# Expert matrices loaded with consecutive rows on a partition, in an eight-stage soft-MoE behind two graph convolutions

## The chip, the core and the metric

One core of one Trainium2 chip runs the whole program. The metric is the device time of one execution in microseconds (us). Engines are TensorE (PE; its weight loads are shown apart as PEld), VectorE (DVE), ScalarE (ACT), GpSimd (POOL) and SyncE (SP), which here only issues transfers. Transfers run on the core's 16 DMA engines.

## The reference

Two graph convolutions (6250 nodes, 768 channels, 100000 edges and the self loops), then a soft mixture of experts. The part around the change, cut from the reference:

```python
d_w = jax.nn.softmax(logits, axis=-1)                       # over the 32 slots of an expert
c_w = jax.nn.softmax(logits.reshape(b, l, E * S), axis=-1)  # over all 1024 slots
slots = jnp.einsum('bld,bles->besd', xn, d_w)
h = jax.nn.gelu(jnp.einsum('besd,edh->besh', slots, w1) + b1[:, None, :], approximate=False)
eo = jnp.einsum('besh,ehd->besd', h, w2) + b2[:, None, :]
return jnp.einsum('bkd,blk->bld', eo.reshape(b, E * S, d), c_w)
```

There are E = 32 experts of S = 32 slots. w1 is 32 x 768 x 384 and w2 is 32 x 384 x 768, both float32: 1.18 MB for each matrix of each expert, 75.5 MB together.

## The kernel before

The program runs in phases with a barrier between them: `prepare`, `constants`, `first_layer` (first convolution), `second_layer` (second convolution, logits, both softmaxes, sums of the slots), `experts` and `combine`. Rows of 128 nodes make a block; there are 49 blocks (NBR).

**second_layer.** Per block PE does 17 steps of four matmuls for the convolution (line 1370: 512 and 256 columns in turn, weights `pick[:, i % 2, :, t]`, read with a stride of 18 float16 elements, 36 bytes), 36 matmuls for the logits (line 1398), 12 transposes (lines 1414 and 1422) and, for the sums of the slots, six units (line 1385, `unit(n)`). A unit makes one 128 x 512 piece of `slots` for two blocks: six matmuls of 512 columns whose weights are 128 columns of the normalised rows `xn`. There are 12 units for each of 24 pairs of blocks, and 12 shorter ones for the last block, 300 in all. DVE adds each result to `slots` (line 1257). `slots[p, c, k]` holds channel d = c * 128 + p of slot k, since the unit for chunk c takes the columns c * 128 to c * 128 + 127 of `xn`. Units stand between the steps of the convolution, so nearly always behind a matmul of 256 columns.

**Loads of the first four experts.** SP issues w1 of experts 0 to 3 in round NBR + 1 of its loop (line 1168) and w2 of experts 0 to 3 behind the loop (line 1183).

**experts.** Four experts (G) make a group; there are eight groups. Per group PE does `up` (line 1545: 24 matmuls of float32 by w1, on 32 columns of the array each), three transposes of the activated `hb` (line 1553) and `down` (line 1562: 24 matmuls by w2). Up of group i is placed ahead of the transposes and down of group i - 1. ACT's order is: scaled slots `sl`, Gelu of group i (line 1504), copy `hT` of group i - 1 (line 1508). DVE adds the first bias for group i (line 1522) and the second for group i - 1 (line 1526).

The loads come from SP alone, in this order for group i: four first biases (line 1480), four second biases (line 1483), four w1 of group i + 1 (line 1472, once up of group i - 1 has freed the buffer), then, once down of group i - 1 is done (w2 has one buffer), four w2 of group i (line 1490). A bias is one row of HBM that is written to 32 partitions. All of these go through one queue in order, so the biases of group i + 1 lie behind w2 of group i.

w1 of one expert is loaded as `"(c p) h -> p c h"`: six pieces of 384 float32 (1536 bytes) for each partition. w2 is loaded as `"(c p) d -> p c d"`: three pieces of 768 float32 (3072 bytes).

**combine** multiplies the experts' outputs by the combine weights, 49 blocks of 48 matmuls.

Of the kernel before, what the change touches and what calls it, by code (L numbers as in the profile page):

```python
# [12 lines left out]
P = 128  # L13
# [3 lines left out]
DC = D // P  # L17
# [19 lines left out]
HC = H // P  # L37
# [1018 lines left out]
                    steps(14, CT)  # L1056


def second_layer(nc, table, idx, dloc, tab, dinv_g, brow, valid, phi_h, phi_l, scl, slots, ident16, iota_x, x_pad, x2_dram, cw_dram,
                 rows_mem, sums_mem, w1, w2, w1_first, w2_place, w1_in, w2_in):  # L1060

    with ExitStack() as ctx:
# [6 lines left out]
        def sb(name, shape, dt):  # L1069
            return ctx.enter_context(nc.sbuf_tensor("m_" + name, shape, dt))  # L1070

        RING = 14
        XN = 6
        DW = 4
# [12 lines left out]
        xn = sb("xn", [P, XN, 2, D], F16)  # L1087
# [3 lines left out]
        dw = sb("dw", [P, DW, 2, K], F16)  # L1091
# [15 lines left out]
        ps_s = ctx.enter_context(nc.psum_tensor("m_ps_s", [P, 2, 512], F32))  # L1107
# [40 lines left out]
        with nc.Block() as block:  # L1148
            @block.sync
            def _(sp):  # L1150
                for i in range(NBR + 3):
                    if i < NBR:
                        b = own_block(sp, tab, i)
                        wait(sp, based, 2 * (i - 1))
                        sp.dma_start(own[:, i % 2, :], table[bass.ds(b * P, P), :]).then_inc(self_in[i % 2], 16)
                    j = i - 2
                    if 0 <= j < NBR:
                        b2 = own_block(sp, tab, j)
                        sp.wait_ge(x2_r, j + 1)
                        sp.dma_start(x2_dram[bass.ds(b2 * P, P), :], xb[:, j % 2, :]).then_inc(x2_out[j % 2], 16)  # L1160
                    if i < NBR:
                        wait(sp, xn_f, i - 1)
                        wait(sp, x2_out[i % 2], 16 * (i // 2))
                        sp.dma_start(xb[:, i % 2, :], x_pad[bass.ds(b * P, P), :]).then_inc(x_in[i % 2], 16)
                    if i == NBR + 1:
                        sp.wait_ge(consumed, NT)
                        for q in range(G):
                            sp.dma_start(w1_first[:, q], w1[q].rearrange("(c p) h -> p c h", p=P)).then_inc(w1_in[q], 16)
                    k = i - 3
                    if 0 <= k < NBR:  # L1170
                        b3 = own_block(sp, tab, k)
                        sp.wait_ge(cw_hi, k + 1)
                        sp.wait_ge(cw_lo, k + 1)
                        sp.dma_start(cw_dram[bass.ds(b3 * P, P), :], cst[:, :]).then_inc(cw_out, 16)
                sp.wait_ge(x2_out[0], 16 * ((NBR + 1) // 2))
                sp.wait_ge(x2_out[1], 16 * (NBR // 2))
                sp.wait_ge(evicted, 2 * NBR)
                sp.wait_ge(zeroed, NBR)
                sp.wait_ge(scaled_u, 3 * NBR)
                sp.wait_ge(xn_f, NBR)  # L1180
                sp.wait_ge(xn_lo, NBR)
                for q in range(G):
                    sp.dma_start(w2_place[:, q], w2[q].rearrange("(c p) d -> p c d", p=P)).then_inc(w2_in[q], 16)
                sp.wait_ge(cw_out, 16 * NBR)

            @block.gpsimd
# [168 lines left out]
            @block.tensor  # L1355
            def _(pe):
                for i in range(last):
                    j, k = i - 1, i - 2

                    def steps(first, stop):  # L1360
                        if i >= NBR:
                            return
                        for t in range(first, stop):
                            n = CT * i + t
                            pe.wait_ge(gathered[n % RING], 16 * (n // RING + 1))
                            bit = pe.snap((w >> t) & 1)
                            to = (pe.snap(bit << 9), pe.snap(bit << 8))
                            for half in range(2):
                                for (at, f, e), off in zip(OWN, to):
                                    mm = nc.tensor.matmul(part[:, bass.ds(off + at, e - f)], pick[:, i % 2, :, t],  # L1370
                                                          ring[:, n % RING, half * D + f:half * D + e],
                                                          start=False, stop=(t == CT - 1 and half == 1), skip_group_check=True)
                            mm.then_inc(consumed, 1)

                    def unit(n):
                        g, u = group_unit(i, n)
                        if g is None:
                            return
                        bins = bins_of(g)
                        c, a = u // 2, 512 * (u % 2)  # L1380
                        pe.wait_ge(dw_lo, bins[-1] + 1)
                        wait(pe, added, UNITS * g + u - 1)
                        for q in bins:
                            for xh, dh in ((0, 0), (0, 1), (1, 0)):
                                mm = nc.tensor.matmul(ps_s[:, u % 2, :], xn[:, q % XN, xh, c * P:(c + 1) * P], dw[:, q % DW, dh, a:a + 512],  # L1385
                                                      start=(q == bins[0] and xh == 0 and dh == 0), stop=(q == bins[-1] and xh == 1))
                        mm.then_inc(unit_r, 1)

                    if i < NBR:
                        w = pe.value_load(tab[0:1, 4 * i:4 * i + 1], min_val=0, max_val=2 ** CT)  # L1390
                    if 0 <= k < NBR:
                        pe.wait_ge(xt_hi, k + 1)
                        pe.wait_ge(xt_lo, k + 1)
                        wait(pe, lg_r, k)
                        for c in range(DC):
                            for half, ph in ((0, phi_h), (0, phi_l), (1, phi_h)):
                                for a in (0, 512):
                                    mm = nc.tensor.matmul(ps_l[:, a:a + 512], xT[:, half, c * P:(c + 1) * P], ph[:, c, a:a + 512],  # L1398
                                                          start=(c == 0 and half == 0 and ph is phi_h), stop=(c == DC - 1 and half == 1))
                        mm.then_inc(logits, 1)  # L1400
                    if i < NBR:
                        pe.wait_ge(wiped, i + 1)
                        pe.wait_ge(picked, i + 1)
                    steps(0, 2)
                    unit(0)
                    steps(2, 5)
                    unit(1)
                    steps(5, 8)
                    unit(2)
                    if 0 <= j < NBR:  # L1410
                        pe.wait_ge(xn_hi, j + 1)
                        wait(pe, xt_lo, j)
                        for c in range(DC):
                            mm = nc.tensor.transpose(ps_t[:, c * P:(c + 1) * P], xn[:, j % XN, 0, c * P:(c + 1) * P], ident16[:, :])
                        mm.then_inc(hi_turned, 1)
                    steps(8, 11)
                    unit(3)
                    if 0 <= j < NBR:
                        pe.wait_ge(xn_lo, j + 1)
                        pe.wait_ge(xt_hi, j + 1)  # L1420
                        for c in range(DC):
                            mm = nc.tensor.transpose(ps_t[:, c * P:(c + 1) * P], xn[:, j % XN, 1, c * P:(c + 1) * P], ident16[:, :])
                        mm.then_inc(lo_turned, 1)
                    steps(11, 14)
                    unit(4)
                    steps(14, CT)
                    unit(5)


def experts(nc, w1, eb1, w2, eb2, slots, eo, mxs, ident16, w1_first, w2s, w1_in, w2_in):  # L1430


    with ExitStack() as ctx:
# [13 lines left out]
        ident32 = sb("ident32", [P, P], F32)  # L1447
        sl = sb("sl", [P, 2, DC, P], F32)
        hb = sb("hb", [P, 2, H], F32)
        hT = sb("hT", [P, H], F32)  # L1450
        ps_h = ctx.enter_context(nc.psum_tensor("e_ph", [P, 2, 512], F32))
        ps_g = ctx.enter_context(nc.psum_tensor("e_pg", [P, 512], F32))
# [6 lines left out]
        n = NG // 2 + 1  # L1459
        eb1_v = eb1.rearrange("(g j) (o h) -> g j o h", j=G, o=1)  # L1460
        eb2_v = eb2.rearrange("(g j) (o h) -> g j o h", j=G, o=1)
        w1_v = w1.rearrange("e (c p) h -> p e c h", p=P)
        w2_v = w2.rearrange("e (c p) d -> p e c d", p=P)


        with nc.Block() as block:
# [67 lines left out]
            def _(pe):  # L1534
                def body(j):
                    for s in range(2):
# [11 lines left out]
                        if exists(i - 1, NG):  # L1548
# [1 line left out]
                            pe.wait_ge(act_r, i)  # L1550
                            wait(pe, back, i - 1)
                            for c in range(HC):
                                mm = nc.tensor.transpose(ps_g[:, c * P:(c + 1) * P], hb[:, 1 - s, c * P:(c + 1) * P], ident32[:, :])
                            mm.then_inc(turned, 1)
                            pe.wait_ge(back, i)
                            wait(pe, eo_r, i - 2)
# [135 lines left out]
```

## Time and profile before

| | us |
|---|---|
| median of 3 runs | 3592.69 |
| lowest and highest | 3588.29, 3596.18 |
| the profiled execution, its own time | 3595.14 |
| its span | 3593.4 |
| second_layer, logits and sums of slots, about | 1555 to 2966 |
| experts, from the first bias load to the last down | 2967.8 to 3190.3 |
| combine | from 3193 |

The span is what the profiler records between first and last instruction; 1.7 us of the execution lie around it. PE is busy for 88% of the span, the DMA queues with 53.3% and 27.3% of the 16 engines' time. Starts of instructions are counted from the start of the span.

### The profile page before, as it was taken

The page shows a single profiled execution, that of the slowest core. Times are in us where ns is not written, and L with a number is a line of the kernel's source. Part 1 is how long each engine was busy: PE and PEld are TensorE (multiplying, and loading weights), DVE is VectorE, ACT ScalarE, POOL GpSimd, SP SyncE. Part 2 cuts the span into 40 slices and gives each one's busy share as a digit, 9 for nine tenths or more (in the row PEclk, how much of TensorE's full clock was granted, in tenths as well). Part 3 has the DMA queues.
Part 4 walks back from the last instruction along what each step waited for, and adds up shares of the span by engine and source line. Part 5 has one row for each costly group of instructions (what it writes and reads, how often), then busy time and mean ns, then how long its engine had stood idle before and what let it go on. Part 6 is the DMA issues. An engine that isn't in the chain of part 4 may idle for free. (4 is left out here: it accounts for less than half of the span.)

```text
span 3593.4 us, 60125 instructions
## 1 busy us (share of the span) xinstructions
PE 3161.1 (88%) x19503; PEld 1984.9 (55%) x19503; DVE 1954.4 (54%) x2997; ACT 1176.2 (33%) x1414; POOL 1820.1 (51%) x1692
## 2 busy tenths in 40 slices
PE   7214999999999999969999999999999984469998
PEld 6212666666666666635555555555555541136665
DVE  7865444444444444338888888887888870111111
ACT  6662222222222222214444444444444430000000
POOL 0104777777777777467666666666666600000000
PEclk9997999999999999979999999999999997779999
DMA  9364999999999999579888888888888849956665
GB/s 376 123 270 153 323 327 311 307 310 309 304 313 308 306 312 309 198 252 350 300 299 306 305 303 300 299 306 302 305 296 305 304 173 324 354 179 173 164 172 140
DMA packets 360335, 994.09 MB, mean 277 GB/s; under 512 B 139458, under 2 KB 168412, under 8 KB 360080
## 3 DMA queue, kind: packets, MB, share of 16 engines
q0 software_dynamic: 133728, 656.12, 53.3%
q1 hardware_dynamic: 226352, 334.57, 27.3%
q8 instruction: 160, 2.62, 0.3%
q14 instruction: 95, 0.78, 0.1%
HBM read 841.95 MB, written 122.89 MB: 269 GB/s over the span
## 5 line engine op out<-in xcount | busy, mean ns | idle before, releaser
L1191 POOL DMA_INDIRECT rows_mem<-table,idx x833 | 915.1, 1099 | 480.3 <-PE m_part L1370 239.8
L900 POOL DMA_INDIRECT rows_mem<-table,idx x833 | 883.7, 1061 | 346.6 <-issue 179.2
L1370 PE MATMUL m_part<-rows_mem,sums_mem 128*128 128x512 f16 (+1 forms) x3332 | 600.6, 330 | 28.9 <-DMA rows_mem<-table,idx 24.7
L1023 PE MATMUL a_part<-rows_mem,sums_mem 128*128 128x512 f16 (+1 forms) x3332 | 581.2, 328 | 49.0 <-DMA rows_mem<-table,idx 44.4
L1370 PEld LDWEIGHTS m_part<-rows_mem,sums_mem 128*128 128x128 f16 x3332 | 422.6, 142 | 176.5 <-issue 42.7
L1023 PEld LDWEIGHTS a_part<-rows_mem,sums_mem 128*128 128x128 f16 x3332 | 414.1, 142 | 177.3 <-issue 58.3
L1385 PE MATMUL m_ps_s<-m_dw,m_xn 128*128 128x512 f16 x1764 | 429.5, 380 | 28.2 <-DVE slots L1257 26.7
L1398 PE MATMUL m_ps_l<-phi_mem,m_xT 128*128 128x512 f16 x1764 | 388.7, 379 | 0.1
L1665 PE MATMUL c_po<-c_eh,c_cT 128*128 128x512 f16 (+1 forms) x1568 | 320.7, 327 | 7.4 <-DMA c_cT<-cw_dram 7.4
L1398 PEld LDWEIGHTS m_ps_l<-phi_mem,m_xT 128*128 128x128 f16 x1764 | 172.5, 98 | 208.0 <-issue 0.4
L1385 PEld LDWEIGHTS m_ps_s<-m_dw,m_xn 128*128 128x128 f16 x1764 | 167.0, 98 | 214.4 <-issue 56.0
L1004 PE MATMUL a_ps_o<-W1h,a_vT 128*128 128x512 f16 (+1 forms) x1176 | 248.3, 327 | 2.0 <-DVE a_vT L986 2.0
L1004 PE MATMUL a_ps_o<-W2h,a_vT 128*128 128x512 f16 (+1 forms) x1176 | 248.8, 327 | 0.9 <-ACT a_vT L936 0.9
L989 DVE SCALAR_TENSOR_TENSOR a_u<-a_ps_o,inv,brow 128x768 f32<-128x768 f32 x49 | 49.9, 1018 | 331.5 <-PE a_ps_o L1004 331.5
L1648 DVE SCALAR_TENSOR_TENSOR c_ob<-c_po,c_inv,c_xb 128x768 f32<-128x768 f32 x49 | 49.8, 1017 | 330.1 <-PE c_po L1665 330.1
L1257 DVE TENSOR_TENSOR slots<-slots,m_ps_s 128x512 f32<-128x512 f32 x288 | 196.4, 683 | 42.2 <-PE m_ps_s L1385 41.5
L1665 PEld LDWEIGHTS c_po<-c_eh,c_cT 128*128 128x128 f16 x1568 | 153.8, 98 | 110.0 <-DMA c_cT<-cw_dram 7.8
L1197 ACT ACTIVATE m_part<-m_zeros 128x1536 f32<-128x1536 f32 x50 | 72.7, 1453 | 373.5 <-DVE sums_mem L1288 365.2
L1665 PE MATMUL c_po<-c_el,c_cT 128*128 128x512 f16 (+1 forms) x784 | 192.2, 327 | 0.0
L933 ACT ACTIVATE sums_mem<-a_u,dinv_s 128x768 f16<-128x768 f32 x49 | 45.9, 937 | 432.1 <-DVE a_u L989 432.1
L1004 PEld LDWEIGHTS a_ps_o<-W1h,a_vT 128*128 128x128 f16 x1176 | 115.3, 98 | 76.6 <-ACT a_vT L930 2.1
L1004 PEld LDWEIGHTS a_ps_o<-W2h,a_vT 128*128 128x128 f16 x1176 | 115.5, 98 | 75.9 <-issue 1.4
(346 smaller groups left out, 3951.4 us busy)
## 6 DMA issues: line engine op xcount, KB each, us to landing
sums_mem<-table SPq DMA_DIRECT2D x98, 384.0 KB, 6.1
sums_mem<-in_L_ffn_w_dram SPq DMA_DIRECT2D x32, 1152.0 KB, 10.3
rows_mem<-table,idx POOLq DMA_INDIRECT x1666, 5.2
cw_dram<-m_cst SPq DMA_DIRECT2D x49, 512.0 KB, 5.6
x_pad<-xs SPq DMA_DIRECT2D x7, 2688.0 KB, 23.9
table<-arena SPq DMA_DIRECT2D x49, 384.0 KB, 2.7
table<-a_stage SPq DMA_DIRECT2D x49, 384.0 KB, 4.2
sums_mem<-x_pad SPq DMA_DIRECT2D x49, 384.0 KB, 5.0
```

The costliest lines, as they stand in the source:

```text
L900: pool.indirect_dma_start(out=ring[:, t, :], out_offset=None, in_=table, in_offset=bass.IndirectOffsetOnAxis(ap=idx[:, k:k + 1], axis=0)). ...
L989: v.scalar_tensor_tensor(u[:, :], ps_o[:, 0:D], inv[:, 0:1], brow[:, :], ALU.mult, ALU.add).then_inc(biased, 1)
L1004: mm = nc.tensor.matmul(ps_o[:, a:z], vT[:, half, c * P:(c + 1) * P], Wp[:, c, a:z], start=(c == 0 and half == 0 and Wp is Ws[0]), stop=(c ...
L1023: mm = nc.tensor.matmul(part[:, bass.ds(to + a, z - a)], pick[:, i % 2, :, t], ring[:, t, half * D + a:half * D + z], start=False, stop=(t ...
L1191: pool.indirect_dma_start(out=ring[:, t, :], out_offset=None, in_=table, in_offset=bass.IndirectOffsetOnAxis(ap=idx[:, n:n + 1], axis=0)). ...
L1197: nc.scalar.activation(part[:, :], zeros[:, :].to_broadcast([P, 3 * 512]), ACT.Copy).then_inc(wiped, 1)
L1257: v.tensor_tensor(slots[:, c, a:a + 512], slots[:, c, a:a + 512], ps_s[:, unit % 2, :], ALU.add).then_inc(added, 1)
L1370: mm = nc.tensor.matmul(part[:, bass.ds(off + at, e - f)], pick[:, i % 2, :, t], ring[:, n % RING, half * D + f:half * D + e], start=False ...
L1385: mm = nc.tensor.matmul(ps_s[:, u % 2, :], xn[:, q % XN, xh, c * P:(c + 1) * P], dw[:, q % DW, dh, a:a + 512], start=(q == bins[0] and xh ...
L1398: mm = nc.tensor.matmul(ps_l[:, a:a + 512], xT[:, half, c * P:(c + 1) * P], ph[:, c, a:a + 512], start=(c == 0 and half == 0 and ph is phi ...
L1648: v.scalar_tensor_tensor(ob[:, s, :], ps_o[:, s, 0:D], inv[:, 0:1], xb[:, s, :], ALU.mult, ALU.add).then_inc(summed, 1)
L1665: mm = nc.tensor.matmul(ps_o[:, s, a:e], cT[:, s, half * KC + c, :], ee[:, c, a:e], start=(c == 0 and half == 0 and ee is eh), stop=(c == ...
```

## The change

The expert matrices are loaded so that consecutive rows stand on one partition: w1 as `"(p c) h -> p c h"` (partition p holds rows 6p to 6p + 5), w2 as `"(p c) d -> p c d"` (rows 3p to 3p + 2). Either is then one piece of 9216 contiguous bytes in HBM and in SBUF for each partition, in place of six or three. What multiplies w1 and w2 has to stand in the same order: chunk c of `slots` becomes the channels d = 6p + c, and chunk c of the transposed activations the hidden units h = 3p + c. Both come from reading the weights of a matmul with a stride (`spread`): 6 float16 elements (12 bytes) in line 1385, and 3 float32 elements (12 bytes) in the transposes of line 1553. The numbers of matmuls, transfers, bytes and waits stay as they are.

```diff
+def spread(rows, n):
+
+    return rows.rearrange("p (d c) -> p c d", c=n)
 ...
-                            sp.dma_start(w1_first[:, q], w1[q].rearrange("(c p) h -> p c h", p=P)).then_inc(w1_in[q], 16)
+                            sp.dma_start(w1_first[:, q], w1[q].rearrange("(p c) h -> p c h", p=P)).then_inc(w1_in[q], 16)
 ...
-                    sp.dma_start(w2_place[:, q], w2[q].rearrange("(c p) d -> p c d", p=P)).then_inc(w2_in[q], 16)
+                    sp.dma_start(w2_place[:, q], w2[q].rearrange("(p c) d -> p c d", p=P)).then_inc(w2_in[q], 16)
 ...
-                                mm = nc.tensor.matmul(ps_s[:, u % 2, :], xn[:, q % XN, xh, c * P:(c + 1) * P], dw[:, q % DW, dh, a:a + 512],
+                                mm = nc.tensor.matmul(ps_s[:, u % 2, :], spread(xn[:, q % XN, xh, :], DC)[:, c, :], dw[:, q % DW, dh, a:a + 512],
 ...
-        w1_v = w1.rearrange("e (c p) h -> p e c h", p=P)
-        w2_v = w2.rearrange("e (c p) d -> p e c d", p=P)
+        w1_v = w1.rearrange("e (p c) h -> p e c h", p=P)
+        w2_v = w2.rearrange("e (p c) d -> p e c d", p=P)
 ...
-                                mm = nc.tensor.transpose(ps_g[:, c * P:(c + 1) * P], hb[:, 1 - s, c * P:(c + 1) * P], ident32[:, :])
+                                mm = nc.tensor.transpose(ps_g[:, c * P:(c + 1) * P], spread(hb[:, 1 - s, :], HC)[:, c, :], ident32[:, :])
```

## Rows read from the trace of the kernel before

**Rows 1.** The page, 40 equal slices of 89.8 us: PE busy in tenths, GB/s.

```profile
PE   7214999999999999969999999999999984469998
GB/s 376 123 270 153 323 327 311 307 310 309 304 313 308 306 312 309 198 252 350 300 299 306 305 303 300 299 306 302 305 296 305 304 173 324 354 179 173 164 172 140
```

**Rows 2.** Timeline, PE, second_layer: start, length (us), line, operation, count.

```profile
2745.42 2.11 PE L1370 MATMUL m_part<-rows_mem,sums_mem 128*128 128x512 f16 x12
2747.37 1.46 PE L1385 MATMUL m_ps_s<-m_dw,m_xn 128*128 128x512 f16 x6
2748.66 2.11 PE L1370 MATMUL m_part<-rows_mem,sums_mem 128*128 128x512 f16 x12
```

**Rows 3.** Timeline of experts, groups 2 and 3; in brackets the idle time before and its releaser.

```profile
3054.77 3.59 SPq L1490 DMA_DIRECT2D sums_mem<-in_L_ffn_w_dram  x4
3061.59 6.09 PE L1545 MATMUL e_ph<-rows_mem,e_sl 128*32 128x384 f32 x48 [6.89 <-DMA rows_mem<-in_L_ffn_w_dram]
3076.60 0.56 DVE L1522 TENSOR_TENSOR e_hb<-e_ph,e_bias 128x384 f32<-128x384 f32 x1 [19.88 <-DMA e_bias<-in_L_ffn_b_dram]
3078.54 6.15 PE L1562 MATMUL e_pe<-sums_mem,e_hT 128*32 128x512 f32 x48 [10.38 <-ACT e_hT L1508]
3084.75 2.67 SPq L1490 DMA_DIRECT2D sums_mem<-in_L_ffn_w_dram  x4
```

**Rows 4.** Windows of 1 us, experts: busy times, PE's granted clock, DMA share, GB/s.

```profile
3053.00:3054.00 1.00, 1.00 (x16) 0.36 (x12) 0.00 (x0) 0.00 (x0) 0.00 (x0) 1.00 1.06 373
3064.00:3065.00 1.00, 1.00 (x12) 0.45 (x8) 0.00 (x0) 0.00 (x0) 0.00 (x0) 0.50 1.03 399
3072.00:3073.00 1.00, 0.00 (x0) 0.00 (x0) 0.00 (x0) 0.00 (x0) 0.00 (x0) 0.77 1.10 207
3087.00:3088.00 1.00, 0.00 (x0) 0.00 (x0) 0.01 (x1) 0.00 (x0) 0.00 (x0) 1.00 1.02 379
3143.00:3144.00 1.00, 0.00 (x0) 0.00 (x0) 0.87 (x2) 0.00 (x0) 0.00 (x0) 1.00 1.07 217
```

**Rows 5.** Windows of 4 us in prepare and constants: x in, x_pad out, phi in.

```profile
32.00:36.00 4.00, 3.60 (x38) 3.33 (x36) 3.59 (x5) 3.07 (x9) 0.00 (x0) 1.00 1.03 402
84.00:88.00 4.00, 3.65 (x37) 3.36 (x36) 3.62 (x6) 4.00 (x9) 0.00 (x0) 1.00 1.03 417
256.00:260.00 4.00, 0.73 (x1) 0.50 (x2) 4.00 (x1) 3.21 (x1) 0.00 (x0) 1.00 1.03 411
```

**Rows 6.** Timeline of experts: first w2 load, first w1 load within, later w2 issues, last down.

```profile
2947.86 2.48 SPq L1183 DMA_DIRECT2D sums_mem<-in_L_ffn_w_dram  x4
2972.49 4.72 SPq L1472 DMA_DIRECT2D e_w1s<-in_L_ffn_w_dram  x4
3001.24 2.50 SPq L1490 DMA_DIRECT2D sums_mem<-in_L_ffn_w_dram  x4
3141.99 2.17 SPq L1490 DMA_DIRECT2D sums_mem<-in_L_ffn_w_dram  x4
3169.44 2.26 SPq L1490 DMA_DIRECT2D sums_mem<-in_L_ffn_w_dram  x4
3183.87 6.39 PE L1562 MATMUL e_pe<-sums_mem,e_hT 128*32 128x512 f32 x48 [14.01 <-DMA sums_mem<-in_L_ffn_w_dram]
```

**Rows 7.** Weight loads by line; ns are min/median/max.

```profile
L1370 PEld LDWEIGHTS m_part<-rows_mem,sums_mem x3332: 139/141/165, 1555.2 to 2900.1; 128*128 128x128 f16 x196
L1385 PEld LDWEIGHTS m_ps_s<-m_dw,m_xn x1764: 95/98/151, 1657.9 to 2965.1; 128*128 128x128 f16 x196
L407 PEld LDWEIGHTS psT<-ident,work x7: 180/230/230, 12.2 to 13.3; 128*128 128x128 f32 x7
L1553 PEld LDWEIGHTS e_pg<-e_ident,e_hb x24: 138/140/143, 2995.4 to 3169.5; 128*128 128x128 f32 x24
```

**Rows 8.** Timeline, a unit that had to wait: its weight loads and its matmuls.

```profile
2758.57 0.99 PEld L1385 LDWEIGHTS m_ps_s<-m_dw,m_xn 128*128 128x128 f16 x6 [0.77 <-issue]
2758.60 1.46 PE L1385 MATMUL m_ps_s<-m_dw,m_xn 128*128 128x512 f16 x6 [0.46 <-DVE slots L1257]
```

## Prediction

> **What bounds the kernel now.** I read the slices of the page first [rows 1]. The reader should see two regimes: from slice 17 to 32 (second_layer) PE is at nine tenths in nearly every slice at about 300 GB/s, and in slices 34 and 35 (experts) PE falls to four tenths while the rate is the highest behind the start, 324 and 354 GB/s. The change touches both: weight reads in the first, transfers in the second.
>
> In second_layer the timeline of PE [rows 2] shows each group of matmuls starting before the recorded end of the one ahead, with nothing between them. This phase is bound by PE, so anything that a matmul of line 1385 waits for longer would be paid in full.
>
> In experts a period runs from one issue of w2 to the next. In [rows 3] it goes: w2 issued at 3054.77; w1 of the next group arrives at 3061.59; the first bias, queued behind w2, arrives at 3076.60; down starts at 3078.54, once Gelu and the copy `hT` are done; down ends and w2 is issued again at 3084.75. All that time the DMA engines have work (share 1.02 to 1.10 in the windows [rows 4]). Three rates are to be seen there: 373 GB/s while w1 moves (pieces of 1536 bytes), 399 while w2 moves (3072 bytes), and for about 6 us a dip to 207 at its lowest while the biases move. Issues lie at 3001.24 and, six periods on, at 3169.44 [rows 6], so 28.03 us each. A group's w1 and w2 are 4.72 MB each: 4.72 / 0.373 = 12.65 us and 4.72 / 0.399 = 11.8 us, together 24.5; the other 3.5 us are the biases' dip.
>
> **How fast 9 KB pieces move.** No transfer of the trace has such pieces. The nearest rows [rows 5]: x in, 3072 bytes, 402 GB/s; x_pad out, 3072 bytes, 417; phi in, 4096 bytes, 411. A fit helps: one of 16 engines moves 1536 bytes at 373/16 GB/s in 65.9 ns and 3072 bytes at 399/16 in 123.2 ns, that is 8.6 ns for a piece and 0.0373 ns for a byte. It gives 406 GB/s at 4096 bytes (411 measured) and 419 at 9216. The best loads and stores measured are 411 and 417. I take 418, with 411 and 430 as ends (the second is the fit with the cost of a piece at nothing, 16 / 0.0373), and 373 as the low end for the case that a long piece has a cost of its own. At 418 a matrix group takes 11.3 us: w1 saves 1.35 us, w2 saves 0.5.
>
> The Trainium skill (DMA: Bandwidth & Descriptors, Specifications) puts the minimum transfer for line rate at 512 B, by which both old sizes are full speed already and this saves nothing. The rows disagree: 373, 399 and 411 GB/s at three sizes above that. The rule's outcome is the third rival.
>
> **What of it reaches the end.** If only the DMA engines set the period, it falls from 28.03 by 1.85 to 26.2. But there is a second limit, the loop through w2's single buffer: issue, about 1.3 us to the first bytes (my reading of the last period, below), w2, biases, DVE, ACT, down, issue. Now the queue still holds w1 when w2 is issued, so that the loop has slack: w2 issued at 3084.75 finds w1 moving until about 3087, where the rate passes 373 [rows 4]. That is 2.2 us after the issue, so 0.9 us of slack. In the last full period there is none: issue at 3141.99 [rows 6], and the window 3143 to 3144 already dips to 217 GB/s [rows 4]. That period, 3141.99 to 3169.44, is 27.45 us long, and so a sample of the loop; with w2 shorter by 0.5 it is 26.95. The loop varies with down, 6.15 us in [rows 3]: PE's granted clock moves between 0.50 and 1.00 in this stage [rows 4].
>
> So a period lands between 26.2 (DMA alone) and 26.95 (loop alone), against 28.03: 1.1 to 1.8 us each. Six periods give 6.5 to 11; I take 8, since a shorter w1 brings the loop to the front in about every second period. Ahead of them lies w1 of group 1, issued at 2972.49 [rows 6]: 1.35 us from the rate. Issuing it took SP 4.72 us for four transfers of 768 pieces; with 128 pieces each the queue fills sooner, 0 to 1.5 us, taken as 0.7. Behind them is the last w2, issued at 3169.44 and there at 3183.87 [rows 6], nothing beside it: 0.45 us. Sum: 8 + 1.35 + 0.7 + 0.45 = 10.5 us, with ends of 7 and 16. The first loads (lines 1168, 1183) run beside second_layer. The later one is issued at 2947.86 [rows 6], has 11.8 us to move and so is there by about 2962, while experts starts at 2967.8: 0. With less for SP to issue, the biases are issued earlier, but they stay behind w2 in the same queue, so 0 again; nobody else waits on SP, and no wait is added or moved.
>
> **What the strided weights cost.** Loads with a stride of 36 bytes take 141 ns (line 1370), contiguous ones 98 (line 1385) [rows 7]. At 12 bytes I expect at most 141. The question is whether 43 ns more show. Line 1370 itself tells: from 2745.42 to 2747.37 [rows 2] twelve matmuls with strided weights, six of 512 and six of 256 columns, take 1.95 us, 2.36 columns/ns; the unit behind them, six contiguous loads and 3072 columns from 2747.37 to 2748.66, runs at 2.38. So strided loads hide even behind matmuls of 256 columns (107 ns), and a unit's loads lie behind its own matmuls of 512 (215 ns), the first behind one of 256. When a unit had to wait, its matmul began 0.03 us after its load began [rows 8], not after its end. I take 0. The upper bound is 43 ns exposed once in each of 300 units, 12.9 us; nothing lets a slower load gain, so there is no bound below 0.
>
> The Trainium skill (SBUF — State Buffer, Door 1: The DMA port swizzle, its note on cachelines) asks for two or more accesses to each 16-byte line for full bandwidth. Twelve bytes give 1.3 to a line, so by it the loads of line 1385 slow down; the trace agrees for 36 bytes (141 against 98 ns [rows 7]) and shows nothing at 12. What a slower load would do to the time is the fourth rival.
>
> The transposes of line 1553 read float32 with 12 bytes: 24 loads of 140 ns [rows 7]. They follow up, which ends at 3067.7, and ACT copies their result only behind the Gelu that the bias released at 3076.60 [rows 3]; with 8 us of cover the cost is 0. Uncovered, 24 loads at the slowest float32 row (230 ns [rows 7]) would cost 24 x 0.09 = 2.2 us.
>
> **The rivals.**
> 1. *The loop is the bound throughout* (faster, or within 0.2%). Periods of 26.95 and no gain from the quicker issue: 6.5 + 1.35 + 0.45, less where down falls to a lower clock more often: 5 to 8, some 6.5 us, 3586. For it: the last period. Against: slack in the others.
> 2. *The engines are the bound throughout.* 11 + 1.35 + 1.5 + 0.45 = 14.3 us, up to 17 at 430 GB/s: 3578. For it: a DMA share above 1 in all six periods.
> 3. *Longer pieces don't move faster* than now: 3592.7. Against it are three rising rates.
> 4. *The strided weights show once a unit*: +12.9 against -10.5, 3595. Against it: [rows 2] and [rows 8].
> 5. *Slower: a strided load outlasts its matmul.* It decides where a load at this stride, together with what it shares, takes more than the 215 ns of a 512-column matmul. The slowest strided float16 load is 165 ns, a float32 one 230 [rows 7]; at 230 each of 1764 matmuls waits 15 ns, 26 us, less 10.5: 3608. The same sign, smaller, would come from 9 KB pieces at 373 GB/s: w2 then loses 0.85 us in seven groups, 6 us, 3599.
>
> **How the numbers follow.** About 0.2% (7 us) is what a measurement of this kernel can tell from no change. Chances: the forecast 0.45; the loop 0.17; the engines 0.13; no faster pieces 0.08; strides once a unit 0.07; slower 0.10 for its two forms. Faster than by 0.2%: nearly all of the forecast (0.42), all of the engines, a third of the loop, 0.61 in all. Slower by more than 0.2%: 0.09. Within: 0.30. The likeliest change is -10.5 us. Against the profiled execution that is 3595.1 - 10.5 = 3584.6; the three runs' median lies 2.4 us lower, so 3582.2, rounded to 3582. The range runs from the engines' end, 3575, to the fourth rival's 3595.
>
> **What the profile after would show.** In one-microsecond windows of experts, w1 and w2 at the same rate near 418 GB/s; if w1 stays at 373, the whole gain is wrong. Issues of line 1490 every 26.2 to 27 us; short stretches in which the DMA engines run dry right after an issue would say that the loop has taken over. Four w1 issued in about 2 us into an empty queue, and no longer 14 us. Weight loads of line 1385 near 141 ns, with a unit still 1.29 us behind twelve matmuls in 1.95; longer ones would mean the fourth or fifth rival. The prediction fails if a unit stretches by more than 30 ns (300 of them, 9 us), or if the biases' dip grows.

## The result, and the profile after

| us | before | after |
|---|---|---|
| median of six runs each | 3594.43 | 3581.99 |
| lowest and highest | 3587.91, 3597.83 | 3579.13, 3583.24 |
| the profiled execution, its span | 3593.4 | 3580.3 |
| from the first w1 issue in experts to the issue of combine's first load (of the combine weights, on SP) | 220.53 | 206.83 |

The ratio is 0.9967 (95% interval 0.9954 to 0.998), 12.4 us off the medians, 7 to 17 us by the interval. Of all executions reported in this document one is left out, of the experiment a2, which took 5758.5 us at a granted clock of 0.58. All lines of the code behind the new helper have moved down by five: 1385 is now 1390, 1472 is 1477, 1480 is 1485, 1490 is 1495, 1545 is 1550, 1553 is 1558 and 1562 is 1567.

The page of after, the same slices as [rows 1], and one of its groups (line, engine, tile, count; busy us and mean ns; idle before them):

```profile
PE   7214999999999999969999999999999984469998
GB/s 376 125 271 152 327 325 304 310 310 306 309 311 305 310 310 309 215 243 347 298 308 294 305 300 304 303 297 305 302 307 299 298 174 338 382 180 169 166 171 140
...
L1390 PE MATMUL m_ps_s<-m_dw,m_xn 128*128 128x512 f16 x1764 | 433.1, 383 | 27.0 <-DVE slots L1262 26.9
```

Slices 34 and 35 now move 338 and 382 GB/s, against 324 and 354. Nothing else stands out of the noise. The matmuls of the units last 383 ns on average, 380 before.

One period of experts in the timeline of after, to be laid beside [rows 3]:

```profile
3051.22 2.06 SPq L1495 DMA_DIRECT2D sums_mem<-in_L_ffn_w_dram  x4
3055.86 5.77 PE L1550 MATMUL e_ph<-rows_mem,e_sl 128*32 128x384 f32 x48 [4.71 <-DMA rows_mem<-in_L_ffn_w_dram]
3069.57 0.56 DVE L1527 TENSOR_TENSOR e_hb<-e_ph,e_bias 128x384 f32<-128x384 f32 x1 [16.40 <-DMA e_bias<-in_L_ffn_b_dram]
3071.51 6.61 PE L1567 MATMUL e_pe<-sums_mem,e_hT 128*32 128x512 f32 x48 [9.34 <-ACT e_hT L1513]
3078.18 1.96 SPq L1495 DMA_DIRECT2D sums_mem<-in_L_ffn_w_dram  x4
```

It has the same shape. w2 is issued, up starts, the bias arrives late, down runs and w2 is issued again. The period is 26.96 us here, and was 29.98 in [rows 3]. Windows of the same period (busy times of PE, PEld, DVE, ACT, POOL; PE's granted clock; DMA share; GB/s), as [rows 4]:

```profile
3054.00:3063.00 9.00, 6.31 (x51) 2.84 (x51) 0.00 (x0) 0.00 (x0) 0.00 (x0) 0.81 1.01 427
3063.00:3067.00 4.00, 0.00 (x0) 0.00 (x0) 0.00 (x0) 0.00 (x0) 0.00 (x0) 0.93 1.05 300
3078.00:3079.00 1.00, 0.12 (x4) 0.00 (x0) 0.60 (x1) 0.00 (x0) 0.00 (x0) 1.00 0.18 74
3079.00:3080.00 1.00, 0.00 (x0) 0.00 (x0) 0.87 (x2) 0.00 (x0) 0.00 (x0) 1.00 0.93 184
```

The first is w2: 427 GB/s, where w2 ran at 399 and w1 at 373. The second is the biases' dip, which is still there. The last two are new. Right after the issue of 3078.18 the engines had nothing to do for most of a microsecond: w2 was issued too late to follow w1. There the loop through its buffer was in front.

Issues of w1 and w2 (the two of w2 in the timeline above left out), as [rows 6]:

```profile
2972.88 2.12 SPq L1477 DMA_DIRECT2D e_w1s<-in_L_ffn_w_dram  x4
2998.81 1.97 SPq L1495 DMA_DIRECT2D sums_mem<-in_L_ffn_w_dram  x4
3024.07 1.75 SPq L1495 DMA_DIRECT2D sums_mem<-in_L_ffn_w_dram  x4
3057.13 1.86 SPq L1477 DMA_DIRECT2D e_w1s<-in_L_ffn_w_dram  x4
3103.21 1.75 SPq L1495 DMA_DIRECT2D sums_mem<-in_L_ffn_w_dram  x4
3129.98 1.75 SPq L1495 DMA_DIRECT2D sums_mem<-in_L_ffn_w_dram  x4
3156.55 1.99 SPq L1495 DMA_DIRECT2D sums_mem<-in_L_ffn_w_dram  x4
```

The first up had been, before:

```profile
2988.89 6.60 PE L1545 MATMUL e_ph<-e_w1s,e_sl 128*32 128x384 f32 x48 [14.32 <-DMA e_w1s<-in_L_ffn_w_dram]
```

and after, with the last down:

```profile
2986.72 6.34 PE L1550 MATMUL e_ph<-e_w1s,e_sl 128*32 128x384 f32 x48 [13.48 <-DMA e_w1s<-in_L_ffn_w_dram]
3170.19 6.76 PE L1567 MATMUL e_pe<-sums_mem,e_hT 128*32 128x512 f32 x48 [13.14 <-DMA sums_mem<-in_L_ffn_w_dram]
```

Six periods lie between 2998.81 and 3156.55, so one is 26.29 us (28.03 before). One by one they are 25.26, 27.15, 26.96, 25.03, 26.77 and 26.57 us. Four w1 take SP 2.12 and 1.86 us to issue.

The whole difference can be laid out by place. In us: the two convolutions up to second_layer's first weight load, 1555.2 before and 1552.7 after, -2.5 (nothing there was changed, so this is chance between two executions); second_layer, 1409.9 and 1412.8, +2.9; w1 issue to combine's first load, -13.7; combine, +0.2. Sum -13.1, the difference of the spans. What the change itself did in this pair is about -10.6.

### The profile page after: what moved, and what is told of

It reads as the page before. It is cut to its first block and busy times, and to the rows that moved or that the text cites. A ratio compares the mean times of both kernels' runs of the same rounds, so it can differ in the third digit from the quotient of the medians.

```text
span 3580.3 us, 60125 instructions
## 1 busy us (share of the span) xinstructions
PE 3158.8 (88%) x19503; PEld 2030.0 (57%) x19503; DVE 1955.0 (55%) x2997; ACT 1176.3 (33%) x1414; POOL 1822.3 (51%) x1692
## 5 line engine op out<-in xcount | busy, mean ns | idle before, releaser
L1390 PE MATMUL m_ps_s<-m_dw,m_xn 128*128 128x512 f16 x1764 | 433.1, 383 | 27.0 <-DVE slots L1262 26.9
L1390 PEld LDWEIGHTS m_ps_s<-m_dw,m_xn 128*128 128x128 f16 x1764 | 211.3, 126 | 178.0 <-issue 55.7
```

Of the source, the lines that this page charges most:

```text
L1390: mm = nc.tensor.matmul(ps_s[:, u % 2, :], spread(xn[:, q % XN, xh, :], DC)[:, c, :], dw[:, q % DW, dh, a:a + 512], start=(q == bins[0] an ...
```

## The experiments

The times of each group of experiments are read against runs of the kernel before on the same chip. "The change" is the kernel after.

### The two matrices apart

a1 has the new w1 loads and the strided units that go with them; w2 and the transposes are as before. a2 is the rest.

```diff
 a1_w1_only, against the change
-                    sp.dma_start(w2_place[:, q], w2[q].rearrange("(p c) d -> p c d", p=P)).then_inc(w2_in[q], 16)
+                    sp.dma_start(w2_place[:, q], w2[q].rearrange("(c p) d -> p c d", p=P)).then_inc(w2_in[q], 16)
...
-        w2_v = w2.rearrange("e (p c) d -> p e c d", p=P)
+        w2_v = w2.rearrange("e (c p) d -> p e c d", p=P)
...
-                                mm = nc.tensor.transpose(ps_g[:, c * P:(c + 1) * P], spread(hb[:, 1 - s, :], HC)[:, c, :], ident32[:, :])
+                                mm = nc.tensor.transpose(ps_g[:, c * P:(c + 1) * P], hb[:, 1 - s, c * P:(c + 1) * P], ident32[:, :])
```

> Only w1 is loaded in 9216-byte pieces, with the strided weights of line 1385 that this needs; w2 and the transposes as before. Loop or engines, whichever is later (mine): at 424 GB/s w1 needs 11.1 us in place of 12.65, the head gains 2.5 us, six periods about 0.9 us each, -8 us in all against the kernel before, and the DMA engines run dry after some issues of w2. Engines alone: 1.5 us in each of six periods and 2.5, -11.5 us. Loop alone: periods stay, -2.5 us. With a visible cost of the strides each is 2 to 13 us worse.

> Only w2 is loaded in 9216-byte pieces, with the strided transposes; w1 and line 1385 as before. w2 needs 11.1 us in place of 11.8. It stands on the loop and on the engines' sum alike, so mine, the loop alone and the engines alone all say seven times 0.7, -5 us; windows with w1 stay at 373 GB/s. If the transposes' strided float32 loads (201 ns against 140) mattered, the gain would be under 4 us.

Measured: a1 3586.38 us, ratio 0.9976 (0.9967 to 0.9985), -8.4 us; a2 3589.4, 0.9986 (0.9976 to 0.9995), -5.3. From the first w1 issue to combine's first load a1 takes 210.6 us (-9.9) and a2 216.6 (-4.0). The mean period between w2 issues is 26.90 us in a1 and 27.54 in a2. The stage's gains add up to 13.9, and the change shows 13.7, so the two halves don't share a limit. w1 brings more than twice what w2 brings: its pieces were half as long, and the head is nearly all its own (28.75 us from the first w1 issue to the first w2 issue before, 25.86 in a1, 28.33 in a2).

### Strides without the pieces, and pieces without the strides

a3 leaves all loads as before and keeps the strided reads; a4 has the new loads and contiguous reads. In both, rows of w1 and w2 meet the wrong channels, so they compute another function with the same work.

```diff
 a4_pieces_only, against the change
-                                mm = nc.tensor.matmul(ps_s[:, u % 2, :], spread(xn[:, q % XN, xh, :], DC)[:, c, :], dw[:, q % DW, dh, a:a + 512],
+                                mm = nc.tensor.matmul(ps_s[:, u % 2, :], xn[:, q % XN, xh, c * P:(c + 1) * P], dw[:, q % DW, dh, a:a + 512],
```

> Both strided weight reads, all loads as before; rows of w1 and w2 then meet the wrong channels, so this computes another function at the same work. Hidden strides (mine): 0 to +3 us against the kernel before, all of it in units that had to wait for a result on VectorE and in the last block, 0.02 us each. Strides once a unit: +27 ns on each of 300 units, +8 us. Weight loads of line 1385 at 125 ns.

> All loads in 9216-byte pieces, all weight reads contiguous as before; channels meet the wrong rows, another function at the same work. Hidden strides (mine): -12 to -15 us against the kernel before, the change's own gain or up to 3 us more. Strides once a unit: -20 us, since 8 us of the gain went into second_layer.

Measured: a3 3594.51 us, ratio 1.0 (0.9991 to 1.0009); a4 3579.86, 0.9962 (0.9949 to 0.9976), -14.9 us. The group of the units' matmuls in each (a3 first), and all weight loads of that line (ns, min/median/max), in a3 also those of line 1375:

```profile
L1390 PE MATMUL m_ps_s<-m_dw,m_xn 128*128 128x512 f16 x1764 | 432.4, 382 | 30.3 <-DVE slots L1262 29.1 <-DVE slots L1259 0.7
L1375 PEld LDWEIGHTS m_part<-rows_mem,sums_mem x3332: 139/141/166, 1554.4 to 2901.7; 128*128 128x128 f16 x196
L1390 PEld LDWEIGHTS m_ps_s<-m_dw,m_xn x1764: 124/125/152, 1656.0 to 2968.3; 128*128 128x128 f16 x196
```

```profile
L1390 PE MATMUL m_ps_s<-m_dw,m_xn 128*128 128x512 f16 x1764 | 429.1, 380 | 29.3 <-DVE slots L1262 28.2 <-DVE slots L1259 0.5
L1390 PEld LDWEIGHTS m_ps_s<-m_dw,m_xn x1764: 95/98/152, 1656.7 to 2965.3; 128*128 128x128 f16 x196
```

Line 1375, which nobody touched, reads 141 ns as in [rows 7]. Line 1390 reads 125 strided and 98 contiguous. The times of whole kernels can't tell the stride's cost from nothing. The busy time of the line's matmuls, whose ends are modelled, differs by 3.3 us in this pair, but it spreads as much by itself: 430.8 us in c3 and 433.1 in the change, which are one kernel. Over the profiled executions named below it is 428.9 to 429.5 contiguous and 429.6 to 433.1 strided, means 429.2 and 431.5.

The length of second_layer from its first weight load to the last unit's tells more, over nine profiled executions, all but the four of the next section. Contiguous: 1409.9 (before), 1410.2 (a2), 1410.5 (a4). Strided: 1412.8 (the change), 1413.7 (a1), 1413.9 (a3), 1412.6, 1414.1 and 1413.1 (c1, c2 and c3, further down). The means are 1410.2 and 1413.4, and no value of one kind lies among the other. The strides cost 3.2 us, 11 ns for each of 300 units.

### What is left of a period: the biases

The periods of the change still have the biases' dip, 300 GB/s over four microseconds in the windows above. b1 takes the broadcast away: each group's biases come as four rows (18 KB), and a matmul with a matrix of zeros and ones adds them in PSUM, where the matmuls of up and down add up their results.

```diff
 b1_bias_matmul, against the change
+                                sp.dma_start(bias1[0:G, s, :], eb1[bass.ds(i * G, G), :]).then_inc(b1_in[s], 16)
...
+                            nc.tensor.matmul(ps_h[:, s, 0:H], pick_row[:, :], bias1[:, s, :], start=True, stop=False, skip_group_check=True)
```

b2 divides the piece of w1, to 4608 bytes. b3 leaves out two of down's three chunks, b4 the loads of the biases from the third group on; both compute another output.

> The changed kernel, with the biases loaded once per group as four rows on four partitions (18 KB in place of 590 KB written to 128 partitions) and added by a matmul with a matrix that picks the row, ahead of up and of down. If the biases' dip costs 3.5 us a period (mine), the period falls from 26.3 us to the engines' floor, 2 x 4.72 MB at 424 GB/s = 22.3 us: six periods save 24, the head about 3 and the last wait for the bias behind w2 about 5, some -30 us against the changed kernel, 3551. Rival: the dip is only the bias bytes (0.59 MB, 1.4 us a period) and the loop through down holds the rest: -10 us.

> The changed kernel with w1 in two pieces of 4608 bytes a partition (chunk c holds channels 384 a + 3 p + b, weights of the units with a stride of 6 bytes). A fixed cost of 9.5 ns a piece, from 373 GB/s at 1536 and 424 at 9216 bytes, gives 413 GB/s in windows with w1 and 0 to +2 us against the changed kernel. Rival, full speed from 4 KB on: 424 GB/s and no change. Weight loads of the units below 125 ns if the stride sets their length.

> The changed kernel with a third of the matmuls of down (two of three chunks left out, so another output): the loop is some 4 us shorter, the transfers are the same. If the loop still sets a part of the periods, as the dry stretch behind the issue at 3078.18 says, the mean falls from 26.29 to the engines' floor of 25.8 us and no window behind an issue is dry: -3 us, and -4 more for the last two downs, which nothing covers. If the engines alone set it, 26.3 stays. If the loop alone did, 22 us.

> The changed kernel with biases loaded for groups 0 and 1 only and used again for the rest (another output): nothing of the biases in the queue afterwards. Dip costs 3.5 us a period (mine): the mean period falls to 22.3 us, DMA engines never below 400 GB/s between the second w1 and the last w2. Bytes only: 24.9 us.

These four ran on a second chip, on which the kernel before takes 3821.42 us (3815.2 to 3829.68, 18 runs) and the gathers of the convolutions move 269 GB/s over 400 to 1400 us, where the other chips have 310. w2 moves there at the same 424 GB/s, so periods of experts are compared with those of the change on the other chips, and only they are. The change itself was not run on this chip; b2 is the nearest to it there.

**b2.** 3807.06 us, ratio 0.9958 (0.9944 to 0.9972). Windows in which only w1 moves, then only w2:

```profile
3274.00:3281.00 7.00, 6.39 (x48) 1.88 (x48) 0.54 (x1) 0.63 (x1) 0.00 (x0) 0.66 1.02 411
3284.00:3290.00 6.00, 4.96 (x42) 2.23 (x46) 0.00 (x0) 0.00 (x0) 0.00 (x0) 0.72 1.01 427
```

411 GB/s at 4608 bytes, 427 at 9216. The period is 26.44 us. Expected were 413 GB/s and 0 to 2 us lost against the change; six periods of 26.44 us against 26.29 are 0.9.

**b3.** A single execution. The first and the last of seven issues in its timeline:

```profile
3231.09 1.75 SPq L1495 DMA_DIRECT2D sums_mem<-in_L_ffn_w_dram  x4
...
3387.66 1.98 SPq L1495 DMA_DIRECT2D sums_mem<-in_L_ffn_w_dram  x4
```

Six periods with a mean of 26.09 us. Down is down to a third of its work, and behind every issue but the last the rate stays above 400 GB/s, so the loop isn't the limit. The dips stay. The engines give 26.1 us, and the loop adds only 0.2 to reach the mean of the change. 25.8 was expected.

**b4.** A single execution, 3787.78 us. Issues of w2 five periods apart (with no biases between, the second row takes in the next four loads of the same line too), and one window of 40 us:

```profile
3229.18 1.89 SPq L1495 DMA_DIRECT2D sums_mem<-in_L_ffn_w_dram  x4
3339.33 25.11 SPq L1495 DMA_DIRECT2D sums_mem<-in_L_ffn_w_dram  x8
3250.00:3290.00 40.00, 21.72 (x166) 7.97 (x166) 4.94 (x6) 3.27 (x6) 0.00 (x0) 0.78 1.01 423
```

A period of 22.03 us at 423 GB/s throughout. The biases are 0.59 MB of a group's 10.0 MB, 1.4 us at that rate, and they cost 4 us of all 16 engines (26.09 in b3, on the same chip). Whether that comes of the one row that goes to 32 partitions or of the eight small transfers was not told apart.

**b1.** 3817.07 us, ratio 0.9991 (0.9977 to 1.0004), period 27.43: the broadcasts are gone, and the period is longer than the change's, where 22.3 was expected. Its timeline of SP, of PE, and a window behind down's start:

```profile
3250.96 1.88 SPq L1493 DMA_DIRECT2D sums_mem<-in_L_ffn_w_dram  x4
3252.89 0.37 SPq L1484 DMA_DIRECT2D e_bias<-in_L_ffn_b_dram  x1
3278.17 1.98 SPq L1493 DMA_DIRECT2D sums_mem<-in_L_ffn_w_dram  x4
```

```profile
3264.68 1.62 PE L1546 MATMUL e_ph<-e_bias,e_pick_row 128*128 128x384 f32 x2 [13.78 <-DMA e_bias<-in_L_ffn_b_dram]
3266.23 5.40 PE L1552 MATMUL e_ph<-e_w1s,e_sl 128*32 128x384 f32 x48
3271.56 1.56 PE L1559 MATMUL e_pe<-e_bias,e_pick_row 128*128 128x512 f32 x4
3274.03 4.08 PE L1571 MATMUL e_pe<-sums_mem,e_hT 128*32 128x512 f32 x48 [0.58 <-ACT e_hT L1512]
```

```profile
3276.00:3279.00 3.00, 2.11 (x28) 0.65 (x20) 0.82 (x1) 0.00 (x0) 0.00 (x0) 1.00 0.00 0
```

The bias is a few KB, but it is issued behind w2 (3250.96, 3252.89) in the same queue. Up can now not start before it, and waits 13.78 us for it at 3264.68, until w2 has landed. Down's bias and down follow (3271.56, 3274.03). Up and down, which ran beside the transfers, run one after the other behind w2, and the engines move nothing for 3 us. Before, only DVE's addition behind up waited for the bias.

### The bias in its place

c1 is b1 with the first bias of the next group issued right behind its w1, and the second bias right ahead of w2. c2 has that order with the old broadcasts, so that it tells the order from the cost. c3 is the change again, on the same chip.

```diff
 c1_bias_matmul_ahead, against b1
+                                load_bias1(i + 1, 1 - s)
...
+                            load_bias2(i, s)
```

> As b1_bias_matmul, but the first bias of group i + 1 is queued with w1 of group i + 1 and the second of group i right ahead of w2 of group i, so up no longer waits behind w2. If b1's missing gain was that order (mine): up starts when w1 has landed, no dry stretch, period 22.3 us in place of b1's 27.4; with the head and the last periods -30 us against the changed kernel. Rival, the two passes over the bias rows on TensorE hold the loop: the period stays above 26.

> The changed kernel with its 128-partition bias loads, only queued in that other order. The dips stay, so the engines' floor stays near 26 us a period (mine): 0 to -2 us from six periods, and -4 at the last ones, where down of group 6 no longer waits for a bias behind w2. -3 to -6 us against the changed kernel. If the order and not the dip had cost the 3.5 us a period: -25 us.

> The changed kernel itself, beside the other two on the same chip: 0.33% below the kernel before, as measured at first, if the gain doesn't hang on the chip.

| us (four runs of c1, five of c2 and c3) | median | ratio to before (3592.64) | 95% | period |
|---|---|---|---|---|
| c1 | 3557.68 | 0.9899 | 0.9884 to 0.9914 | 22.34 |
| c2 | 3580.86 | 0.9963 | 0.9949 to 0.9976 | 26.15 |
| c3 | 3579.07 | 0.9961 | 0.9947 to 0.9974 | 26.30 |

c1 in its timeline of SP and PE, and over 40 us:

```profile
2999.78 1.99 SPq L1502 DMA_DIRECT2D sums_mem<-in_L_ffn_w_dram  x4
3133.81 2.03 SPq L1502 DMA_DIRECT2D sums_mem<-in_L_ffn_w_dram  x4
3025.11 1.62 PE L1555 MATMUL e_ph<-e_bias,e_pick_row 128*128 128x384 f32 x2 [5.12 <-DMA e_bias<-in_L_ffn_b_dram]
3036.90 4.08 PE L1580 MATMUL e_pe<-sums_mem,e_hT 128*32 128x512 f32 x48 [3.44 <-DMA sums_mem<-in_L_ffn_w_dram]
3020.00:3060.00 40.00, 22.13 (x166) 8.61 (x170) 4.94 (x6) 3.49 (x6) 0.00 (x0) 0.86 1.01 421
```

Up now waits for a bias that lands right behind its w1, 421 GB/s are moved throughout, and c1 is 35.0 us faster than before and 21.4 faster than the change. That is the best version here. It falls short of what was expected by 8.6 us. Six periods of 22.34 against 26.30 make 23.8. The rest of the expectation was 5 us at the end of experts, which six periods had in part counted already, and the head became longer: the first w2 is issued 28.5 us after w1 (2971.27 to 2999.78), 25.9 in the change, and the engines stand still ahead of it:

```profile
2996.00:2998.00 2.00, 2.00 (x32) 0.85 (x28) 0.00 (x0) 0.01 (x1) 0.00 (x0) 1.00 0.02 9
```

c2's timeline and windows tell why the order alone brings nothing:

```profile
3023.24 1.70 SPq L1487 DMA_DIRECT2D e_bias<-in_L_ffn_b_dram  x4
3024.98 1.85 SPq L1504 DMA_DIRECT2D sums_mem<-in_L_ffn_w_dram  x4
```

```profile
3026.00:3029.00 3.00, 0.00 (x0) 0.02 (x1) 0.00 (x0) 0.00 (x0) 0.00 (x0) 0.50 1.11 243
```

The second bias moves when it is issued, ahead of w2, and the rate drops to some 240 GB/s then instead of later. The dip has moved, and the period of 26.15 says that it has not shrunk. c2 lies 1.8 us above c3 where 3 to 6 less were expected, within what the intervals can tell.

## Why the prediction was right

The forecast was 3582 us, and 3581.99 was measured. That it fits to the last digit is luck: the forecast took 10.5 us off a median of three runs, 3592.69, where the six of before have 3594.43, and 12.4 us is the measured gain. Two readings of [rows 1] were off, and nothing rests on them: slice 17 still belongs to first_layer, and slice 19 moves 350 GB/s, more than slice 34. By its steps:

**Rate of a 9 KB piece.** 418 GB/s predicted, with the fit at 419; measured 424 (windows of 415 to 442). Right, and slightly low. With b2 there are four sizes in the same stage: 373, 399, 411 and 424 GB/s at 1536, 3072, 4608 and 9216 bytes. One engine of 16 takes 65.9, 123.2, 179.4 and 347.8 ns for a piece. The line through the first and the last has a slope of 0.0367 ns a byte and 9.5 ns for the piece; at 4608 bytes it gives 178.6, where 179.4 was measured. The full rate was not reached at 1536 bytes, as the third rival would have it. w1 saves 1.5 us a group (1.35 in the sum), w2 0.67 (0.5).

**Six periods.** -8 predicted, -10.5 measured (168.20 us, now 157.74). Both limits are there, as told. The last period is the loop's in any case, since no w1 is left to move ahead of its end. This window lies in it, and nothing moves while PE runs down:

```profile
3148.00:3156.00 8.00, 6.24 (x44) 2.27 (x48) 0.48 (x1) 0.90 (x2) 0.00 (x0) 0.55 0.00 0
```

It takes 26.57 us, 27.45 before, and 26.95 was expected. The loop had set it before too: the DMA share of that period was 0.62 then, so the second rival's share above 1 in all six periods held in five.

The other five went from a mean of 28.15 us to 26.23, -1.92. The loop was to be in front in about every second period. Behind two of their issues, 3051.22 and 3078.18, the rate does fall below 250 GB/s for a microsecond. But that costs little: the rates alone would save 2.2 us, so what the loop takes back is some 0.3 us a period. b3 agrees, where the loop is out of the way and the first five periods have a mean of 26.10. The length of a single period doesn't tell its limit, since the number of bytes between two issues varies: 9.2 MB in the 25.03 us behind 3078.18, 10.2 MB in the 26.77 behind 3103.21.

Of the 2.5 us that were missing in the forecast, 0.7 was lost in the working itself, since six periods halfway between 26.2 and 26.95 are -8.7, and -8 was taken. Most of the rest is the engines' term, which was mis-sized: the rates save 2.2 us a period and not 1.85, 1.6 us in five periods.

**Head.** -1.35 from the rate and -0.7 from the issue predicted. From w1's issue to the start of up it was 16.40 us before and is 13.84 now, -2.56. SP needs 2.12 us for four w1 where it needed 4.72.

**Tail.** -0.45 predicted, and -0.42 measured up to combine, in part by luck. From the last issue of w2 to the last down it was 14.43 us before and is 13.64 now, -0.79; down itself was longer, 6.76 against 6.39.

**Strides.** Taken as 0, measured +3.2 us in six executions against three. This step failed, if by little. Its rows were right: a unit behind twelve matmuls still starts 1.95 us after them and gives way 1.30 us later, as in [rows 2]:

```profile
2744.78 2.11 PE L1375 MATMUL m_part<-rows_mem,sums_mem 128*128 128x512 f16 x12
2746.73 1.46 PE L1390 MATMUL m_ps_s<-m_dw,m_xn 128*128 128x512 f16 x6
2748.03 2.11 PE L1375 MATMUL m_part<-rows_mem,sums_mem 128*128 128x512 f16 x12
2757.50 1.48 PE L1390 MATMUL m_ps_s<-m_dw,m_xn 128*128 128x512 f16 x6 [0.19 <-DVE slots L1262]
```

The step said that a slower load hides even where a unit waited, since its matmul began 0.03 us after the load began [rows 8]. The last line above is such a unit, and takes 1.48 us, where [rows 8] has 1.46. Its first load has no matmul ahead of it to hide behind, and some 20 ns of the 27 that a load grew by show. How often that happens stands in the view of line 1390, in what PE sat idle for before it (us, times):

```profile
  DVE slots L1262: 26.9, 53
```

53 times 20 ns is 1.1 us, a third of the 3.2. Where the rest arises is not shown.

The loads themselves became slower, 98 to 125 ns; at most 141 were expected. No load came near the 215 ns of a matmul of 512 columns (153 at most), so the fifth rival's point was not reached, and its other form fell with the rate of 424 GB/s.

**Transposes.** 201 ns a load and not 140, and nothing of it reaches the end: three take 0.62 us against 0.55, behind a bias that is 8 us late. The cost of 0 was right, and the cover is the one that was named:

```profile
L1558 PEld LDWEIGHTS e_pg<-e_ident,e_hb x24: 188/201/215, 2993.0 to 3156.7; 128*128 128x128 f32 x24
```

The Trainium skill (SBUF — State Buffer, Door 1: The DMA port swizzle, its note on cachelines) has loads slow down below two accesses to a 16-byte line. The rows agree in direction for both lines at 12 bytes, 98 to 125 ns in float16 and 140 to 201 in float32. They don't agree with the strides that the same note calls free, up to 8 elements of bf16 and 4 of float32: here 6 and 3 elements were read. What a slower load would have meant for the time, the fourth rival's 12.9 us, came to a quarter of that.

**The sum.** -10.5 predicted; measured -13.7 in experts (the six periods 10.5, the head up to the first w2 issue 28.75 - 25.93 = 2.8, the tail 0.4) and +3.2 in second_layer. So the forecast is as near as it is because a gain that was 3.2 us too small met a cost that was 3.2 us too small, and that is luck. The 12.4 us of the medians are 1.9 more than this sum, well within their interval.

What stays open: where two thirds of the strides' 3.2 us arise, whether fewer waits of units would bring back the other third (1.1 us), and what the head of c1 could be with its first biases issued elsewhere; none of these was tried.

## What to carry to other kernels

Where a stage is limited by its transfers, read the rate of each piece size in windows of its own and fit a cost for the piece and one for the byte; this gave a size outside the fit within 2%. Layouts of weights for long pieces cost little if the reordering can go into a weight read that hides behind 512 columns, but count the places where PE had waited, and measure the stage: here 3.2 us of it showed all the same. And look for the small transfer that is slow for its bytes: 0.59 MB of broadcast rows cost 4 us where 4.72 MB cost 11; taking it away only paid once what replaced it had left the place behind a large transfer in its queue.

## What was not expected of the hardware

- Loads of HBM rows that are each written to 32 partitions were far slower than their bytes: eight of them, 0.59 MB, took 4 us of all 16 engines, and 1.4 us at the rate of the matrices (b4 against b3).
- The time of a weight load grew with its stride: in float16 98 ns for contiguous columns, 103 at 6 bytes (b2), 125 at 12 and 141 at 36.
- One chip gathered at 269 GB/s where the others had 310, and took 6% longer for the whole kernel, with long contiguous loads at the same 424 GB/s.
